# An attention reordered, its value sums copied out by ScalarE and divided by GpSimd

## What is computed

```
x = x + tanh(g_xattn[0]) * align(ctx, layernorm(x))          # dynamic time warping
x = x + tanh(g_ffn[0])   * moe0(layernorm(x))                # 64 experts, top 8
x = x + tanh(g_xattn[1]) * attention(layernorm(x), ctx, ctx) # 16 heads of 8, 77 keys
x = x + tanh(g_ffn[1])   * moe1(layernorm(x))                # 8 experts, top 2
```

## Time and profile before

| | us |
|---|---|
| median of three runs | 821.64 (821.53 to 822.69) |
| the profiled execution | 821.36 |
| its span, first instruction to last | 819.6 |
| attention, first scores to last reciprocal's start | 488.2 to 577.9 |
| last layer norm and router, to the first gate matmul | 577.9 to 595.3 |
| second feed-forward at its even pace, from | 608.3 |

### The profile page before, as it was taken

How to read it: one execution, slowest core, us unless ns; L and a number is a source line. 1 busy time by engine, 2 the same in 40 slices (tenths; PEclk the granted TensorE clock), 3 DMA queues, 4 the chain that set the end, 5 groups by cost and what they waited for, 6 DMA issues and landing times.

```text
span 819.6 us, 13449 instructions
## 1 busy us (share of the span) xinstructions
PE 660.4 (81%) x3450; PEld 504.2 (62%) x3450; DVE 616.1 (75%) x2015; ACT 387.3 (47%) x688; POOL 402.7 (49%) x403
## 2 busy tenths in 40 slices
PE   5653320088999999999999958887699999999995
PEld 2321110076788788888888735554578888888884
DVE  6689999777777777777777684676676777777774
ACT  3533110035565555656565641233355656555663
POOL 5358750026566666666666560000136666666663
PEclk9655555558999999999999956999689999999998
DMA  5534431104887776777777300000117757566661
GB/s 139 77 85 135 138 108 33 36 1 103 159 162 143 148 156 141 155 136 159 139 158 145 72 1 9 2 2 2 36 26 148 160 133 162 131 161 143 153 142 52
DMA packets 73602, 85.89 MB, mean 105 GB/s; under 512 B 38954, under 2 KB 51611, under 8 KB 70489
## 3 DMA queue, kind: packets, MB, share of 16 engines
q1 hardware_dynamic: 66506, 75.05, 44.1%
q0 software_dynamic: 4320, 9.68, 4.1%
q10 hardware_dynamic: 2734, 0.69, 0.4%
HBM read 76.69 MB, written 8.70 MB: 104 GB/s over the span
## 4 chain that ended last, share of the span: by engine, by line
PE 68%; DVE 23%; issue 4%; DMA 2%; ACT 1%; POOL 1%; DVEq 0%; POOLq 0%; ACTq 0%
PE bank L990 7%; PE bank L992 7%; PE bank L991 7%; PE bank_quad L1144 7%; PE bank_pair L990 6%; PE bank_pair L992 6%; PE bank_pair L991 6%; PE bank_quad L1142 6%; PE bank_quad L1141 6%; PE bank L1070 3%; DVE arena L1430 3%; PE bank_pair L1029 2%; DVE rden L1563 2%; DVE arena L1426 2%; DVE arena L1387 2%
## 5 line engine op out<-in xcount | busy, mean ns | idle before, releaser
L673 POOL TENSOR_TENSOR act_lo<-arena,act_hi 128x512 fp32r<-128x512 f32 x232 | 301.2, 1298 | 193.7 <-ACT act_hi L837 192.8
L1657 DVE TENSOR_TENSOR bank_pair<-arena,bank_pair 128x512 f32<-128x512 f32 x220 | 152.5, 693 | 103.1 <-ACT arena L851 71.8
L851 ACT ACTIVATE arena<-bank 128x512 f32<-128x512 f32 x232 | 138.7, 598 | 181.2 <-PE bank L992 181.1
L1665 DVE TENSOR_TENSOR arena<-bank_pair,arena 128x512 f32<-128x512 f32 x220 | 152.1, 691 | 13.8 <-DMA arena<-scr_mask 1.5
L837 ACT ACTIVATE act_hi<-arena 128x512 fp32r<-128x512 f32 x232 | 144.6, 623 | 9.8 <-DVE arena L1655 6.5
L594 POOL TENSOR_SCALAR xn<-x_res,mv,rstd 128x128 f32<-128x128 f32 x16 | 14.1, 882 | 169.0 <-DVE rstd L1234 97.7
L1144 PE MATMUL bank_quad<-act_lo,w_hi 128*128 128x512 f32 x232 | 92.8, 400 | 3.3 <-POOL act_lo L673 3.3
L990 PE MATMUL bank_pair<-xn_hi,w_hi 128*128 128x512 f32 x232 | 93.5, 403 | 1.5 <-DVE arena L1655 1.5
L990 PE MATMUL bank<-xn_hi,w_hi 128*128 128x512 f32 x232 | 92.9, 400 | 0.0
L992 PE MATMUL bank<-xn_lo,w_hi 128*128 128x512 f32 x232 | 92.4, 398 | 0.0
L991 PE MATMUL bank<-xn_hi,w_lo 128*128 128x512 f32 x232 | 92.1, 397 | 0.0
(11 more groups left out here) (221 smaller groups left out, 1087.5 us busy)
## 6 DMA issues: line engine op xcount, KB each, us to landing
arena<-scr_mask SPq DMA_DIRECT2D x94, 512.0 KB, 6.8
scr_w<-prep_out POOLq DMA_DIRECT2D x25, 192.0 KB, 2.2
w_raw<-scr_w SPq DMA_DIRECT2D x25, 192.0 KB, 6.4
w_raw<-in_L_ffn_expert_gate_k SPq DMA_DIRECT2D x32, 64.0 KB, 6.1
w_raw<-in_L_ffn_expert_up_k SPq DMA_DIRECT2D x32, 64.0 KB, 5.9
w_raw<-in_L_ffn_expert_down_k SPq DMA_DIRECT2D x64, 32.0 KB, 5.5
prep_in<-in_L_ffn_wg POOLq DMA_DIRECT2D x21, 64.0 KB, 2.3
prep_in<-in_L_ffn_wu POOLq DMA_DIRECT2D x21, 64.0 KB, 2.1
```

The costliest lines, as they stand in the source:

```text
L673: nc.gpsimd.tensor_tensor(act_lo[:, k % 2, :], act_a[:, k % 2, :], act_hi[:, k % 2, :].bitcast(F32), ALU.subtract).then_inc(FF[f]["alo"], 1)
L851: nc.scalar.activation(act_s[:, k % 2, :], ps[4 + k % 2][:], ACT.Silu).then_inc(FF[f]["silu"], 1)
L1657: nc.vector.tensor_tensor(ps[6 + i][:], act_s[:, i, :], ps[6 + i][:], ALU.mult).then_inc(FF[f]["t"], 1)
L1665: nc.vector.tensor_tensor(act_a[:, i, :], ps[6 + i][:], mask[:, j, 512 * k:512 * (k + 1)], ALU.mult).then_inc(FF[f]["act"], 1)
```

## The change

- **Division.** ScalarE copies `ps[4]` (the value products and the sums) into a new pair of SBUF buffers `av_sums` after each unit (`copy_sums`), and `values(u + 1, 0)` waits for that copy. GpSimd then computes the reciprocal as a power, `den ** -1`, by a TENSOR_TENSOR against a broadcast column of minus one, refines it with one Newton step (a product, a TENSOR_SCALAR, a product), and multiplies: five instructions of 128x256 a unit, in place of two of DVE.
- **Maxima.** `copy_most` moves from DVE to ACT.
- **Order.** `scores` runs one step further ahead of DVE's reductions: the first seven use three pairs of banks in turn (`score_bank`), so that they wait only for the reduction three before. `project` comes two units after its values instead of one.
- **Layer norm 3.** The square root on ACT and the reciprocal go; DVE starts from an integer estimate of the inverse root and takes three Newton steps (`rsqrt`, four parts). Batches 0 and 1 are normalised and turned inside units 4 to 7 (`TURN3`, `NORM3_BEHIND`), batch 2 right behind the units, batch 3 inside the first chunks of the feed-forward.
- **Feed-forward's start.** `gate_up(0, 0)` comes before `project(7)`, and `gate_up(0, 1)` behind it; `route1` moves two chunks later; `first_lo(1)` moves from before the units into unit 7.

Core of the diff (the function `project` is only moved; `low(3, B - 1)` and `high(3, B - 1)` move likewise into the feed-forward):

```diff
@@ constants and tables
-    ROUTE1_BEFORE = {0: [(1, 0), (2, 1), (2, 2)], 1: [(2, 3)], 2: [(2, 4)], 3: [(2, 5)]}
+    ROUTE1_BEFORE = {2: [(0, 0), (1, 0), (2, 1), (2, 2)], 3: [(2, 3)], 4: [(2, 4)], 5: [(2, 5)]}
+    NORM3_BEHIND = {3: 0, 5: 1, 6: 2, 7: 3}
+    TURN3 = {5: 0, 7: 1}
+        def score_bank(j):
+            return bank_quad[:, 2 * (j % 3) - 2:2 * (j % 3)] if j < 7 and j % 3 else bank_pair
@@ gpsimd
+                def normalise_heads(u):
+                    num, den = av_sums[:, u % 2, 0], av_sums[:, u % 2, 1]
+                    pool.wait_ge(s_inv, 4 * u + 1)
+                    if u >= 1:
+                        pool.wait_ge(s_nrm, u)
+                    pool.wait_ge(s_nd, u + 1)
+                    nc.gpsimd.tensor_tensor(rden[:], den, minus_one[:].broadcast_to([P, UTOK]), ALU.pow).then_inc(s_inv, 1)
+                    pool.wait_ge(s_inv, 4 * u + 2)
+                    nc.gpsimd.tensor_tensor(rerr[:], den, rden[:], ALU.mult).then_inc(s_inv, 1)
+                    pool.wait_ge(s_inv, 4 * u + 3)
+                    nc.gpsimd.tensor_scalar(rerr[:], rerr[:], -1.0, 2.0, ALU.mult, ALU.add).then_inc(s_inv, 1)
+                    pool.wait_ge(s_inv, 4 * u + 4)
+                    nc.gpsimd.tensor_tensor(rden[:], rden[:], rerr[:], ALU.mult).then_inc(s_inv, 1)
+                    pool.wait_ge(s_inv, 4 * u + 5)
+                    if u >= 2:
+                        pool.wait_ge(s_wo, u - 1)
+                    nc.gpsimd.tensor_tensor(avT[:, u % 2, :], num, rden[:], ALU.mult).then_inc(s_nrm, 1)
+                for u in range(UNITS):
+                    normalise_heads(u)
+                    if u in NORM3_BEHIND:
+                        normalise(3, NORM3_BEHIND[u])
@@ scalar
+                def copy_sums(u):
+                    act.wait_ge(s_av, RCH * (u + 1))
+                    if u >= 2:
+                        act.wait_ge(s_nrm, u - 1)
+                    nc.scalar.activation(av_sums[:, u % 2].rearrange("p d t -> p (d t)"), ps[4][:], ACT.Copy).then_inc(s_nd, 1)
+                copy_most(0)
                 for u in range(UNITS):
-                    for c in range(RCH):
-                        exp(u, c)
+                    exp(u, 0)
+                    if u >= 1:
+                        copy_sums(u - 1)
+                    exp(u, 1)
+                    exp(u, 2)
+                    if u + 1 < UNITS:
+                        copy_most(u + 1)
+                    if u in TURN3:
+                        high(3, TURN3[u])
@@ tensor, the units
                 for u in range(UNITS):
                     scores_by_key(u, 0)
-                    ahead(4 * u + 6)
                     if u >= 1:
                         values(u - 1, 2)
+                    ahead(4 * u + 7)
                     scores_by_key(u, 1)
-                    ahead(4 * u + 7)
                     values(u, 0)
+                    ahead(4 * u + 8)
                     scores_by_key(u, 2)
-                    ahead(4 * u + 8)
-                    values(u, 1)
-                    if u >= 1:
-                        project(u - 1)
+                    if u >= 2:
+                        project(u - 2)
                     if u + 1 < UNITS:
                         max_back(u + 1)
                     ahead(4 * u + 9)
+                    if u in TURN3:
+                        pe.wait_ge(s_exp, RCH * (u + 1))
+                        turn(3, TURN3[u])
+                    values(u, 1)
+                    ahead(4 * u + 10)
@@ vector, add_unit
                     dve.wait_ge(s_wo, u + 1)
+                    if u + 3 < UNITS:
+                        dve.wait_ge(s_mc, u + 4)
```

More of the change, by code:

```diff
@@ L1010, in logits, with project @@
                 mm.then_inc(s_logit, 1)
+            def project(u):
+                pe.wait_ge(s_nrm, u + 1)
+                if u >= 1:
+                    pe.wait_ge(s_au, u)
+                for t in range(PAIR):
+                    mm = nc.tensor.matmul(ps[5][:, P * t:P * (t + 1)], avT[:, u % 2, P * t:P * (t + 1)], w4[:, 3, :],
+                                          start=True, stop=True)
+                mm.then_inc(s_wo, 1)
             def attention():
@@ L1086, in ahead @@
                         scores(j)
-                for j in range(5):
+                pe.wait_ge(s_xhi, 3 * B)
+                for j in range(6):
                     scores(j)
@@ L1155, in feed_forward @@
                     logits(0, 2)
+                    logits(0, B - 1)
+                for k in range(2):
+                    wait_low(pe, 2 * f + 1, k)
+                    if f == 1 and k == 0:
+                        pe.wait_ge(s_nd, UNITS)
+                    if f == 1 and k == 1:
+                        project(UNITS - 1)
+                        logits(1, 2)
+                        pe.wait_ge(s_au, UNITS)
+                    gate_up(0, k, 0)
+                if f == 0:
+                    pe.wait_ge(s_xhi, 2 * B)
+                    pe.wait_ge(s_score, B)
                 else:
                     turn(3, B - 1)
[L1158 to L1167, removed]
+                    logits(1, B - 1)
                 for u in range(2, CHUNKS * PEEL):
@@ L1588, in attention @@
                 split_most(0)
-                most_of(4)
-                copy_most(0)
-                most_of(5)
+                for j in range(4, 7):
+                    most_of(j)
                 for u in range(UNITS):
-                    ahead(4 * u + 6)
-                    if u >= 1:
-                        normalise_heads(u - 1)
                     ahead(4 * u + 7)
@@ L1598, in attention @@
                         split_most(u + 1)
+                    if u == 4:
+                        rsqrt(0, 0)
+                    if u == 5:
+                        normalise(3, 0)
+                    if u == 6:
+                        low(3, 0)
+                    ahead(4 * u + 8)
+                    if u == 4:
+                        rsqrt(0, 1)
+                    if u == 6:
+                        for part in range(4):
+                            rsqrt(1, part)
+                        normalise(3, 1)
@@ L1599, in attention @@
+                    if u == 7:
+                        first_lo(1)
+                    ahead(4 * u + 9)
                     if u >= 2:
                         add_unit(u - 2)
+                    if u == 4:
+                        rsqrt(0, 2)
+                    ahead(4 * u + 10)
+                    if u >= 2:
                         unit_stats(u - 2)
-                    ahead(4 * u + 8)
-                    if u + 1 < UNITS:
-                        copy_most(u + 1)
-                    ahead(4 * u + 9)
@@ L1619, in attention @@
-                for b in range(B - 1):
-                    mean_var(b)
+                    if u == 4:
+                        rsqrt(0, 3)
+                for part in range(4):
+                    rsqrt(2, part)
+                normalise(3, 2)
+                low(3, 1)
                 add_unit(UNITS - 2)
                 unit_stats(UNITS - 2)
-                normalise_heads(UNITS - 1)
-                last_norm(0)
+                done(nc.vector.memset(wsel[1], 0.0))
+                low(3, 2)
@@ L1625, in attention @@
                 add_unit(UNITS - 1)
                 unit_stats(UNITS - 1)
-                mean_var(B - 1)
-                last_norm(1)
-                low(3, 0)
-                last_norm(2)
-                done(nc.vector.memset(wsel[1], 0.0))
-                low(3, 1)
-                last_norm(B - 1)
-                low(3, 2)
-                route1(0, 0)
+                for part in range(4):
+                    rsqrt(B - 1, part)
+                normalise(3, B - 1)
             def feed_forward(f):
@@ L1678, in feed_forward @@
                             turn0(B - 1)
+                        if f == 1 and u == 2:
+                            low(3, B - 1)
                         if f == 1 and u in ROUTE1_BEFORE:
```

132 lines of the change are left out of this document (61 added, 71 removed).

## The result

Measured side by side, the changed kernel takes 1096.3 us (1095.69 to 1098.45, four runs) and the kernel before 822.16 us (821.53 to 822.87, four runs): 1.334 times as long [1.3315, 1.3362]. That is far above the predicted 834.5 us and above the top of the range, 875. The profiled execution took 1095.69 us, its span 1093.6.

A forecast was written before the change was run, and what follows sets the result against it. A unit was taken as bound by a loop through DVE and PE. Filling -4.7, units +9.2, added pieces and a first unit at half clock +1, end +7.4 sum to +12.9 us: from 821.64 to 834.5 us, range 804 to 875.

The forecast's parts named there:

- Filling: Before the units: first seven scores no longer take turns with the reduction; first scores_by_key at 496.3, gain 4.7 us.
- A unit if nothing else came in: One attention unit, by PE's own list: 7.4 us instead of 9.69, alone saving 16 us over seven units.
- What POOL's instructions cost: POOL's division in each unit: power 5 us, TENSOR_SCALAR 1.6, three products 2.2, handing on 0.2, together 9.0 us.
- What POOL's work does to DVE: In each unit DVE's split waits for POOL's whole power p: unit 6.0 + p, 11.0 us; seven steps +9.2 us.
- The end: From the last value group to the feed-forward's even pace: 39.0 us against 31.6, +7.4 us.
- Each microsecond of p counts 8 times: Each microsecond of the power's length p above 1.4 counts about 8 times: seven units and once at the end.
- It turns at p = 3.4: The power's length, 3.4 us or 13 ns a column, at which the case turns between faster and slower.
- The power is much dearer: Rival: POOL's power takes 8 us or more; 858 us at 8, 874 at 10; chance 0.18.
- the split is not held up: Rival: a power leaves DVE its way, POOL's 9.0 us a unit binds from unit 3; 813 us, chance 0.05.
- The power is cheap: Rival: POOL's power takes under 3.2 us; about 810 us in the middle, chance 0.33.

The follow-up runs named there:

- kernel with the product: Changed kernel with a product of the same shape in place of POOL's power, the reciprocal left out: 798.64 us, 0.972 times before.
- kernel with 64 columns: Changed kernel with the power over 64 of the 256 columns and a product over the other 192: 853.86 us, 1.0391 times before.
- two-step kernel: Changed kernel with an integer reciprocal estimate and two Newton steps, the first with fitted constants, on POOL in place of the power: 802.84 us, ratio 0.9761.

## Why the prediction was wrong, step by step

**Filling: right.** Predicted a gain of 4.7 us with the first `scores_by_key` at 496.3; it starts at 495.7, and the filling is 12.2 - 6.3 = 5.9 us shorter. (Before, it had started at 500.4 and not at the 501.0 that the prediction read; the scores began 1.2 us later in the changed kernel.)

**A unit if nothing else came in: right in kind, 0.4 short.** Predicted 7.4 us, PE's own list. The kernel with the product has 7.81 with PE 97% busy. Seven times 0.4 are 2.9 us of the 16 it was to save; the units are 76.6 - 62.8 = 13.8 us shorter there.

**What POOL's instructions cost: the step that failed.** The three products were right (0.72 against 0.73). The TENSOR_SCALAR was taken from a row of another form (882 ns for 128 columns with an operand for each partition) as 1.6 us; with constants over 256 columns it takes 0.405. That also takes away the ground of the 5 us: two steps were to cost 6.9 ns a column against 2.9 for one, but this TENSOR_SCALAR does two steps for 0.405/256 = 1.6 ns. The power was chosen at 5 us and bounded at 10; it takes 41.13. The upper bound was built as three stages of four passes each "as dear as a product". No row supported such a count: it put a number on an unknown operation by the number of its textbook steps. 41.13 / 0.61 is 67 products (0.61 us: the product in the power's own place). An honest upper end would have been open, and with 8 us of the whole for each microsecond an open end decides.

**What POOL's work does to DVE: wrong.** That the split waits for the whole power was the term that carried the predicted loss of the units. The split takes 0.19 us inside every power that it met, six times in the changed kernel, and 0.60 inside a product. The earlier trace rows showed products only, and the rival that said so got 0.05. The Trainium skill, "SBUF — State Buffer", section "Who interferes with whom", has the lock on the shared ports held for a whole instruction. By that rule a split inside a power of 41 us would last until its end. The traces agree for products of 0.74 and 1.89 us and disagree for the power. By how far this term moved the forecast: without it a power of 5 us leaves POOL's chain at 9.0 us a unit by the prediction's own prices, below the 9.69 of before, and the forecast is the rival's 813.

**The unit with its real price.** Without the hold-up POOL's own five instructions bind, 44.15 us. From the first unit to the last values lie six such steps, since `project` comes two units later: 6 x (44.15 - 9.69) = 206.8 us; measured 205.3.

**The end: right in form.** The prediction counted two powers behind the last values, what is left of unit 6's and all of unit 7's, and put `turn(3,3)` 26.5 us behind them. With the measured prices that is 26.5 + 2 x 36.1 - 2 x 1.2 - 2.6 = 93.7 us. (The 2.6 was POOL's wait for `rsqrt(2)` behind a split held up; POOL's timeline has no such wait.) Measured: 868.32 - 777.6 = 90.7, by PE's timelines of the changed kernel and, second, of the kernel before:

```profile
868.32 1.35 PE L976 MATMUL bank_quad<-ident,xn 128*128 128x128 f32 x4
```

```profile
590.97 1.12 PE L923 MATMUL bank_quad<-ident,xn 128*128 128x128 f32 x4
```

Behind the turn the prediction put 12.5 us "as long as before"; before, it is 608.3 - 590.97 = 17.3 us to the even pace. So its sum holds a gain of 4.8 us there that it doesn't account for. Measured from the turn to the end of the program it is 225.3 against 228.6 us, 3.3 less. Sum of the three with the right price: -4.7 + 206.8 + (7.4 + 72.2 - 2.4 - 2.6) = +276.7 us, where the traces differ by 274.0. The ways through the program were followed rightly in the main, and one duration undid the result.

**Each microsecond of p counts 8 times: right.** 7.9 measured. **It turns at p = 3.4: wrong**, with the hold-up gone. From the kernel with 64 columns back along that rate, 853.9 - 821.5 = 32.4 us is 4.1 us of power: it would turn near 10.5 - 4.1 = 6.4 us, some 40 columns. That is worked out, not run.

**The rivals.** "The power is much dearer", 8 us or more (0.18), is the case that came; its price went to 874 at 10 us and so far missed. Its loss came by POOL's own chain, the mechanism of "the split is not held up" (0.05). "The power is cheap" (0.33) was argued from DVE's reciprocal being 4.2 of its products; that ratio says nothing of a power on POOL.

## What to carry to other kernels

An operation that no trace shows has no upper bound in its textbook steps. Measure it alone on a small tile first; where a loop multiplies its price by eight, leave the range open until then. Keep the order and change the arithmetic: the same reorder is worth 2.4% with eight cheap POOL instructions in place of one power, and the integer start plus two fitted Newton steps is such a form. To find what a change is worth without its suspect, put a product of the same shape in its place; that one run separated a gain of 23 us by the rest of the change from the power's cost of 297.

## What the runs showed of the hardware that was not expected

- A POOL TENSOR_TENSOR with a power takes 41.1 us over 256 columns and 10.5 over 64, about 160 ns a column, for 128 partitions or 8, for exponents -1 and 2 (the latter over 64 columns only), and for constant operands (likewise). A product of 128x256 with the same broadcast operand takes 0.61 us, one of 128x1024 takes 1.89.
- A running power leaves DVE its way: split products of 0.19 us in all six cases inside a power of the changed kernel, and in the kernels with shorter powers. The one exception seen is a cast of 0.52 us that starts 0.12 us behind the first power over 8 partitions; what held it is open. A running product holds DVE to its end: 0.60 us, and for a cast with a single SBUF input 1.26 us. It goes the other way too: in the kernel with the product, a DVE TENSOR_TENSOR of 128x512 that runs from 560.45 to 561.13 makes POOL's product of 560.52 last 1.08 us in place of 0.61. Why a power differs was not settled; that it touches SBUF only now and then would explain it, and no run shows that.
- A DVE cast is held like a product with two inputs. The Trainium skill, "SBUF — State Buffer", section "Who interferes with whom", counts casts among what can take the shared ports, if their operands meet certain conditions; the traces agree, 0.18 us alone and 0.61 inside a 0.73 us product in the two-step kernel.
- The power's length varies by 0.12% (41116 to 41165 ns) while DVE, ACT and PE work beside it or stand; none of them was seen to lengthen it by more.
